# A decoder's last layer on flat tiles of 128 rows instead of 16 sequences of 112

## The reference

```
x = x + L1_attn(layernorm(x))
x = x + L1_xattn(layernorm(x), ctx)     # "wide attention"
x = x + L1_ffn(layernorm(x))            # "the MLP"

L1_xattn: q, k_new, v_new = x wq^T, x wk^T, x wv^T        (512 x 512 each)
          k = [ctx ; k_new], v = [ctx ; v_new]            (375 + 112 rows)
          softmax(q k^T / sqrt(512)) v wo^T               # one head, no mask
L1_ffn:   quant(W) = clip(round(W / s), -1, 1) * s,  s = mean|W| + 1e-8
          (silu(x Wup^T) * (x Wgate^T)) Wdown^T           # hidden width 2048
```

## Time and profile before

| | us |
|---|---|
| median of 3 runs | 3541.77 (3539.74 to 3544.45) |
| profiled execution, span from first to last instruction | 3554.0 |
| wide attention, one step | 19.1 |
| last DVE and POOL work of wide attention | ends 3192.99 |
| first DVE work of the MLP | 3193.34 |
| first block load of the MLP issued | 3199.74 |
| first up matmul of group 0, 1, 2, 3 | 3201.99, 3297.56, 3381.18, 3464.80 |
| last down begins | 3545.33 |

### The profile page before, as it was taken

One profiled execution on the slowest core, in us unless ns is written; L12 is line 12 of the kernel. 1 busy time (PEld: TensorE's weight loads), 2 busy tenths in 40 slices (PEclk: granted clock), 3 DMA queues, 4 the chain that ended last, 5 costly groups with the idle time before them and its releaser, 6 DMA issues. The chain is left out here.

```text
span 3554.0 us, 51327 instructions
## 1 busy us (share of the span) xinstructions
PE 3272.3 (92%) x17848; PEld 2662.8 (75%) x17848; DVE 2392.2 (67%) x6178; ACT 1727.0 (49%) x4171; POOL 794.8 (22%) x941
## 2 busy tenths in 40 slices
PE   5858999997999999999999988999889889988999
PEld 4647877885877877778788767888778667767887
DVE  5997878776666666766676665999655555558332
ACT  5975454444343344534433432888447655541222
POOL 0004444542222222422222213000413400000000
PEclk9879999999999999999999999999989989999999
DMA  6131010001000001100000026999700133423000
GB/s 232 30 67 25 1 48 24 1 36 66 23 26 23 23 23 50 68 21 21 30 21 23 18 92 213 390 400 400 272 22 2 48 125 121 123 88 107 11 10 21
DMA packets 117131, 297.27 MB, mean 84 GB/s; under 512 B 41888, under 2 KB 45472, under 8 KB 111120
## 3 DMA queue, kind: packets, MB, share of 16 engines
q1 hardware_dynamic: 110720, 276.39, 22.1%
q0 software_dynamic: 6160, 17.67, 1.6%
HBM read 251.65 MB, written 41.68 MB: 83 GB/s over the span
## 5 line engine op out<-in xcount | busy, mean ns | idle before, releaser
L42 PE MATMUL bank<-w,cross_ctx_part 128*125 128x512 f32 x1536 | 519.5, 419 | 2.8 <-DVE cross_kn L1176 2.8
L42 PEld LDWEIGHTS bank<-w,cross_ctx_part 128*125 128x125 f32 x1536 | 283.1, 187 | 84.4 <-DVE cross_kn L1176 8.7
L1084 ACT ACTIVATE cross_prob<-bank,cross_neg_max 112x375 f32<-112x375 f32 x256 | 147.3, 575 | 347.6 <-DVE cross_neg_max L1182 347.6
L42 PE MATMUL bank<-w_low,cross_ctx_part 128*125 128x512 f32 x768 | 303.0, 395 | 0.0
L1182 DVE TENSOR_REDUCE cross_neg_max<-bank 112x1 f32<-112x375 f32 x256 | 134.3, 526 | 208.8 <-PE bank L944 205.7
L42 PE MATMUL bank<-moe_wt,moe_zT 128*128 128x448 f32 x1176 | 263.7, 373 | 0.6 <-DVE moe_wt L1869 0.6
L1869 DVE TENSOR_TENSOR moe_wt<-moe_raw,moe_wt 128x1792 fp32r<-128x1792 f32 (+1 forms) x111 | 231.7, 2108 | 15.4 <-ACT moe_wt L1764 14.2
L42 PEld LDWEIGHTS bank<-moe_wt,moe_zT 128*128 128x128 f32 x1176 | 214.8, 189 | 15.9 <-DVE moe_wt L1869 0.8
L42 PE MATMUL bank<-mlp_zT,mlp_signs 128*128 128x448 f32 x1024 | 220.6, 368 | 5.6 <-DVE mlp_zT L2568 5.6
L42 PE MATMUL bank<-w,self_xq 128*128 128x512 f32 (+1 forms) x464 | 195.9, 422 | 23.0 <-DVE w_low L598 21.7
L42 PEld LDWEIGHTS bank<-mlp_zT,mlp_signs 128*128 128x128 f32 x1024 | 193.4, 189 | 27.3 <-issue 5.9
(11 more groups left out here) (433 smaller groups left out, 8171.8 us busy)
## 6 DMA issues: line engine op xcount, KB each, us to landing
moe_raw<-in_moe_w SPq DMA_DIRECT2D x74, 896.0 KB, 7.3
moe_raw<-in_moe_w SPq DMA_DIRECT2D x37, 1024.0 KB, 8.5
stream<-in_L1f SPq DMA_DIRECT2D x32, 768.0 KB, 4.2
cross_ctx_raw<-in_ctxT SPq DMA_DIRECT2D x32, 750.0 KB, 4.2
wide_ctxT<-in_ctxT SPq DMA_DIRECT2D x16, 750.0 KB, 4.2
wide_ctx_rows<-in_ctx SPq DMA_DIRECT2D x16, 750.0 KB
expert_rows<-a_zeros SPq DMA_DIRECT2D x1, 8960.0 KB, 25.7
moe_zrow<-expert_rows SPq DMA_DIRECT2D x35, 256.0 KB, 8.0
```

What stands on the lines that cost most here:

```text
L42: mm = pe.matmul(out, a, b, start=first and n == 0, stop=last and n == len(pairs) - 1)
L1084: op = act.activation(prob[:, t % SLOTS, i, :], score_bank(t)[0:S, i * NK:(i + 1) * NK], ACT.Exp, bias=neg_max[:, h:h + 1], accum_out=tota ...
```

## The change

1. Wide attention no longer measures sequences. SP stores each finished sequence to a tensor in device memory, `x5` of 1792 x 512 (`store_sequence`), and loads it back as tiles of 128 flat rows into slot t of `rows` (`load_tile`), as soon as the last sequence that a tile needs has landed. Tile t overwrites slot t, whose sequence is stored by then.
2. DVE measures tiles 0 to 9 in its steps 5 to 15 (`measure_tile`, three instructions on 128 partitions), four steps after the sequence that completes them. Tiles 10 to 13 (`LATE_TILES`) are measured in the MLP, group 1, step 2 (`measure_late`); POOL roots them there.
3. The MLP has groups of 4, 4, 4 and 2 tiles, that is 512, 512, 512 and 256 columns. Down has 2 matmuls per tile with weights of 128x128. The last store of a sequence and the loads of tiles 11 to 13 stand ahead of the block loads on SP's queue.
4. The loop over groups is written out on all engines, and x is stored as 14 tiles.

```diff
@@ new, beside the layers
+def last_sequence(t):
+    return (SLOT * t + SLOT - 1) // S
+def store_sequence(k, sp, x, b):
+    sp.dma_start(k.x5[S * b:S * (b + 1), :], x[0:S, b, :]).then_inc(k.rows_moved, 16)
+def load_tile(k, sp, x, t):
+    wait(sp, k.tile_landed[t % 2], 16 * (t // 2))
+    sp.dma_start(x[:, t, :], k.x5[SLOT * t:SLOT * (t + 1), :]).then_inc(k.tile_landed[t % 2], 16)
+def wait_tile(k, eng, t):
+    eng.wait_ge(k.tile_landed[t % 2], 16 * (t // 2 + 1))
+LATE_TILES = [t for t in range(NT) if last_sequence(t) + 4 >= B]
@@ wide_attention_layer, SP
                 load_mlp(b)
+                wait(sp, k.rows_moved, 16 * (b - 2))
+                for t in range(NT):
+                    if last_sequence(t) == b - 3:
+                        load_tile(k, sp, rows, t)
+                if b >= 2:
+                    sp.wait_ge(s["x_done"], b - 1)
+                    store_sequence(k, sp, rows, b - 2)
+            sp.wait_ge(s["x_done"], B - 1)
+            store_sequence(k, sp, rows, B - 2)
@@ POOL
-                pool.wait_ge(s["next_vareps"], b + 1)
-                pool.tensor_tensor(k.rstd[0:S, bass.ts(b, 1)], ve[:, bass.ts(b, 1)], k.half[0:S, 0:1], ALU.pow)\
-                    .then_inc(s["next_rooted"], 1)
+                for t in range(NT):
+                    if last_sequence(t) == b - 4:
+                        pool.wait_ge(s["next_vareps"], t + 1)
+                        pool.tensor_tensor(k.rstd[:, t:t + 1], ve[:, t:t + 1], k.half[:, 0:1], ALU.pow)\
+                            .then_inc(k.tile_rooted, 1)
@@ DVE
-            def measure_next(b):
-                dve.wait_ge(s["x_done"], b + 1)
-                dve.bn_stats(stats[:], x[:, b, :]).then_inc(s["next_stat"], 1)
...
+            def measure_tile(t):
+                wait_tile(k, dve, t)
+                dve.bn_stats(stats[:], rows[:, t, :]).then_inc(s["next_stat"], 1)
+                dve.wait_ge(s["next_stat"], t + 1)
+                dve.bn_aggr(k.mean_var[:, t, :], stats[:]).then_inc(s["next_centre"], 1)
+                dve.wait_ge(s["next_centre"], t + 1)
+                dve.tensor_scalar(ve[:, t:t + 1], k.mean_var[:, t, 1:2], EPS, None, ALU.add).then_inc(s["next_vareps"], 1)
...
-                if not first:
-                    measure_next(b - 1)
+                for t in range(NT):
+                    if last_sequence(t) == b - 4:
+                        measure_tile(t)
...
             add_out(B - 1)
-            measure_next(B - 1)
@@ ternary_mlp_layer
-    G = B // GB
+    G = (NT + GB - 1) // GB
+    def tiles_of(g):
+        return range(GB * g, min(GB * (g + 1), NT))
+    def width(g):
+        return P * len(tiles_of(g))
@@ PE: down, up and gate
-                for j in range(GB):
+                for j in range(len(tiles_of(g))):
                     if m == 0:
                         wait(pe, s["x_done"], GB * (g - 1) + j + 1)
-                    mm = product(pe, ps[4 + j][0:S, :], [t[:, m % 2, j * S:(j + 1) * S] for t in hT],
+                    mm = product(pe, ps[4 + j], [t[:, m % 2, j * P:(j + 1) * P] for t in hT],
                                  [signs[:, m, 2 * D:3 * D]], m == 0, m == MC - 1)
...
-                            mm = product(pe, ps[bank + m % 2][:, 0:N], [signs[:, m, at + c * P:at + (c + 1) * P]],
-                                         [t[:, c].rearrange("p b t -> p (b t)") for t in zT], c == 0, c == DC - 1)
+                            mm = product(pe, ps[bank + m % 2][:, 0:width(g)], [signs[:, m, at + c * P:at + (c + 1) * P]],
+                                         [t[:, c, 0:width(g)] for t in zT], c == 0, c == DC - 1)
@@ DVE
+            def measure_late():
+                for n, t in enumerate(LATE_TILES):
+                    wait_tile(k, dve, t)
+                    dve.bn_stats(stats[:, n, :], x[:, t, :]).then_inc(s["stat"], 1)
+                for n, t in enumerate(LATE_TILES):
+                    dve.wait_ge(s["stat"], n + 1)
+                    dve.bn_aggr(k.mean_var[:, t, :], stats[:, n, :]).then_inc(s["centre"], 1)
+                dve.wait_ge(s["centre"], len(LATE_TILES))
+                dve.tensor_scalar(ve[:], k.mean_var[:, LATE_TILES[0]:NT, 1], EPS, None, ALU.add).then_inc(s["vareps"], 1)
...
+                    if g == 1 and m == 2:
+                        measure_late()
@@ POOL, SP
+            pool.wait_ge(s["vareps"], 1)
+            pool.tensor_tensor(k.rstd[:, LATE_TILES[0]:NT], ve[:], k.half[:, 0:len(LATE_TILES)], ALU.pow)\
+                .then_inc(k.tile_rooted, len(LATE_TILES))
...
+            store_sequence(k, sp, x, B - 1)
+            sp.wait_ge(k.rows_moved, 16 * B)
+            for t in LATE_TILES:
+                if last_sequence(t) > B - 4:
+                    load_tile(k, sp, x, t)
             for m in range(MLP_SLOTS, MC):
                 sp.wait_ge(s["sign"], 3 * (m - MLP_SLOTS) + 3)
...
-            with sp.Fori(0, B) as b:
-                sp.wait_ge(s["x_done"], b + 1)
-                sp.dma_start(io["out"][b], x[:, b, :]).then_inc(s["x_stored"], 16)
+            for t in range(NT):
+                sp.wait_ge(s["x_done"], t + 1)
+                sp.dma_start(out[SLOT * t:SLOT * (t + 1), :], x[:, t, :]).then_inc(s["x_stored"], 16)
@@ decoder
-        wide_attention_layer(k, x, io, stream, magnitudes)
-        ternary_mlp_layer(k, x, io, stream, magnitudes)
+        wide_attention_layer(k, x, rows, io, stream, magnitudes)
+        ternary_mlp_layer(k, rows, io, stream, magnitudes)
```

More of the change, by code:

```diff
@@ L61, in __init__ @@
         self.ctx_landed = ctx.enter_context(nc.semaphore("ctx_landed"))
+        self.rows_moved = ctx.enter_context(nc.semaphore("rows_moved"))
+        self.tile_landed = [ctx.enter_context(nc.semaphore(f"tile_landed{i}")) for i in range(2)]
+        self.tile_rooted = ctx.enter_context(nc.semaphore("tile_rooted"))
         self.all_sems = ctx.enter_context(ExitStack())
@@ L2059, in second_attention_layer, with wide_attention_layer @@
         k.next_stage()
-def wide_attention_layer(k, x, io, stream, magnitudes):
+def last_sequence(t):
[8 more added lines that the diff above has]
+LATE_TILES = [t for t in range(NT) if last_sequence(t) + 4 >= B]
+def wide_attention_layer(k, x, rows, io, stream, magnitudes):
     nc, ps = k.nc, k.ps
@@ L2465, in ternary_mlp_layer, with over_loop @@
         half = k.sb(ctx, "mlp_half_scale", [P, 2, 3], F32)
-        z = k.sb(ctx, "mlp_z", [S, GB, D], F32)
-        zT = [k.sb(ctx, f"mlp_zT{i}", [P, DC, GB, S], F32R) for i in range(2)]
-        silu = k.sb(ctx, "mlp_silu", [P, 2, GB * S], F32)
-        h = k.sb(ctx, "mlp_h", [P, 2, GB * S], F32)
-        hT = [k.sb(ctx, f"mlp_hT{i}", [P, 2, GB * S], F32R) for i in range(2)]
-        block = ctx.enter_context(nc.Block())
-        N = GB * S
-        def over_loop(eng, step):
-            step(0, True)
-            with eng.Fori(1, G - 1) as g:
-                step(g, True)
-            step(G - 1, False)
+        z = k.sb(ctx, "mlp_z", [P, GB, D], F32)
+        zT = [k.sb(ctx, f"mlp_zT{i}", [P, DC, GB * P], F32R) for i in range(2)]
+        silu = k.sb(ctx, "mlp_silu", [P, 2, GB * P], F32)
+        h = k.sb(ctx, "mlp_h", [P, 2, GB * P], F32)
+        hT = [k.sb(ctx, f"mlp_hT{i}", [P, 2, GB * P], F32R) for i in range(2)]
+        stats = k.sb(ctx, "mlp_stats", [P, len(LATE_TILES), 6], F32)
+        ve = k.sb(ctx, "mlp_ve", [P, len(LATE_TILES)], F32)
+        block = ctx.enter_context(nc.Block())
+        def over_loop(step):
+            for g in range(G):
+                step(g, g + 1 < G)
         def raw(m, n):
@@ L2527, in _ @@
             pe.wait_ge(s["mean_ready"], 1)
-            over_loop(pe, step)
+            over_loop(step)
         @block.scalar
@@ L2542, in high @@
                         act.wait_ge(s["y_in_psum"], MC * g + m - 1)
-                    act.activation(hT[0][:, m % 2, :], h[:, m % 2, :], ACT.Copy).then_inc(s["h_high"], 1)
+                    act.activation(hT[0][:, m % 2, 0:width(g)], h[:, m % 2, 0:width(g)], ACT.Copy).then_inc(s["h_high"], 1)
                 for m in range(MC):
@@ L2547, in step @@
                     act.wait_ge(s["up_in_psum"], MC * g + m + 1)
-                    act.activation(silu[:, m % 2, :], ps[m % 2][:, 0:N], ACT.Silu, scale=neg_scale[:, 0:1])\
+                    act.activation(silu[:, m % 2, 0:width(g)], ps[m % 2][:, 0:width(g)], ACT.Silu, scale=neg_scale[:, 0:1])\
                         .then_inc(s["silu_ready"], 1)
@@ L2554, in _ @@
             z_high(0)
-            over_loop(act, step)
+            over_loop(step)
         @block.vector
@@ L2584, in low @@
                     dve.wait_ge(s["h_high"], MC * g + m + 1)
-                    dve.tensor_tensor(hT[1][:, m % 2, :], h[:, m % 2, :], hT[0][:, m % 2, :].bitcast(F32),
-                                      ALU.subtract).then_inc(s["h_low"], 1)
-                first = isinstance(g, int) and g == 0
+                    dve.tensor_tensor(hT[1][:, m % 2, 0:width(g)], h[:, m % 2, 0:width(g)],
```

(2 more changed lines are left out.)

56 lines of the change are left out of this document (27 added, 29 removed).

## The result

The changed kernel takes 3519.89 us (median of 4 runs, 3518.53 to 3524.73), the kernel before 3541.13 (3539.74 to 3544.45): ratio 0.9939, 95% interval 0.9928 to 0.9951. That is 21.2 us less; the forecast was 20.9 less, 3520.9.

The account below looks back on a forecast made before the run. PE was taken to bound wide attention and MLP groups 1 to 3, DVE's loop group 0. Terms -1.8, +0.2, +2.4, +1.0, +7.3, +6.2, -34.2, -2.0 sum to -20.9 us: 3541.8 becomes 3520.9, range 3513 to 3530.

Parts of the forecast that it names:

- Step 1: Between the layers: the last sequence's statistics and POOL's root leave the path, -1.8 us.
- Step 2: Wide attention: fewer DVE measurements give no gain, added stores and loads are covered by a step of slack; 0 us.
- rival B: Wide attention: transfers on SP's queue hold up steps 3 to 15, 5.2 us each, +68 us, 3589; 4%.
- Step 3: Start of the MLP: z_low on four tiles is longer, tile loads end in time or nearly so; +0.2 us.
- Step 4: MLP group 0: DVE's loop goes from 5.68 to 5.85 us, +2.4; the last two steps are PE's, +1.0.
- Steps 5 and 6: MLP groups 1 and 2, PE-bound: 512-column matmuls cost 0.0268 us more each; +7.3 and +6.2 us.
- Step 7: MLP group 3: 256-column up and gate -20.0, half the down matmuls -14.8, one PE wait of 0.6; -34.2 us.
- Step 8: The end: two last adds instead of four, -1.5, and one chain at 256 columns, -0.5; -2.0 us.
- The offset of 12.2 us: Profiled span 3554.0 us above the runs' median; taken as the profiled execution's own and carried over.
- Rival A: Group 3: weight loads set the pace, +16.6 us, 3537.5, 4%; load and stream one after the other, 3565, 1%.
- C: Opening of the MLP costs more through PE's slower clock, a late block and PE binding group 0; +6, 3527; 12%.
- D: More is won: wide attention -5, 128-column weights load no slower, boundary shorter by 1 to 2; 3514; 8%.

Follow-up runs that it names:

- measured_at_end: Changed kernel with the statistics of tile 9 taken after the last add_out instead of in step 15; ratio 0.9951 to the kernel before.
- no_moves: Changed kernel without its stores to and loads from device memory and without their waits; ratio 0.9945 to the kernel before.
- moves_twice: Changed kernel with its moves through device memory doubled, all waited for; ratio 0.9943 to the kernel before.
- late_in_group_0: Changed kernel with the statistics of the four late tiles in group 0, step 2, instead of group 1, step 2; ratio 0.9942 to the kernel before.
- small_group_first: Changed kernel with MLP groups in the order 2, 4, 4, 4 tiles; ratio 1.0026 to the kernel before.
- before_written_out: Kernel before with only the loop over the MLP's groups and the loop of stores written out; ratio 1.0006 to the kernel before.
- stores_of_112_rows: Changed kernel with final stores of 112 rows of each tile instead of 128; one run, 3519.34 us.
- one_tile_last: Changed kernel without tile 13 in the last layer, so its last group has one tile and 128-column up and gate matmuls; one run, 3509.93 us.

## Why the prediction was right

The forecast of 3520.9 us was met by 3519.89, and by its own steps. It counts a group from its first up matmul, the table above from its first h. In the changed kernel the first up matmuls stand at 3185.05, 3284.07, 3375.57 and 3466.01; cut there, group 0 is 3.45 us longer than before, group 1 7.9, group 2 6.8, and group 3 up to the last adds 35.75 shorter. The steps are held against these.

- Step 1, the statistics between the layers: -1.8 forecast, -1.85 read. Shown by measured_at_end (+1.66 when put back).
- Step 2, wide attention unchanged: right, shown by no_moves and moves_twice. The landing time in it was mis-sized, 2.6 instead of 11.8 us, and with it rival B's price; its cover held.
- Step 3, start of the MLP: +0.2, read +0.3. SP issued the last tile load at 3182.97 and the first block load at 3183.34, 0.8 us after the signs of block 0; no step of group 0 was longer for it.
- Step 4, group 0: +3.4 forecast, +3.45 read. DVE's loop is 5.86 us for 5.67; the four steps with a normalisation, which the forecast didn't tell apart, are 6.31 for 6.12, the same +0.19. That DVE sets this stage is shown by late_in_group_0 and small_group_first.
- Steps 5 and 6, groups 1 and 2: +13.5 forecast, +14.7 read. Each 512-column matmul was 0.0013 us dearer than forecast and a down matmul with 128 weight columns 0.0026, in all about 1.3 us over the two groups. (The table has +13.5 only because its cut puts the first sixteen matmuls of group 3, which got cheaper, into group 2.) The statistics of the late tiles, 2.9 us of DVE, hid in group 1.
- Step 7, group 3 with step 8's chain: -34.7 forecast, -35.75 read. A matmul of 256 columns at 0.119 instead of 0.1263 and a stall of 0.33 instead of 0.6 us gave 2.2 us more than reckoned. Some 1 us of it was given back at the last step: the down of four matmuls ahead of the last one no longer covers the chain to the last low part, and PE waits 0.56 us before the last down (at 3511.70 above) where it waited 0.19. From the last but one down to the last it is 1.65 us after 2.21, -0.56, where the forecast had counted the shorter down and the shorter chain both, -1.4.
- Both sizes could have been had beforehand. The 0.1263 came by taking 12 x 0.2312 off the whole series of the earlier trace rows, but there the twelve matmuls of 512 columns take from 63.62 to 66.47, 0.2375 each, as the first alone takes 0.34; the twelve of 256 columns, read by themselves, take 1.44 us, 0.120 each. And the chain's terms for the stall, 2.98 + 0.50 + 0.42 + 0.44, come to 4.34 us and not to 4.6, which makes the stall 0.3. PE in order of time, from the first 256-column matmul of that series on, in the kernel before:

```profile
66.47 1.59 PE L42 MATMUL bank<-a_qkv,a_zT 128*128 128x256 f32 x12
67.91 0.39 PE L42 MATMUL bank<-a_o,a_oT 128*128 128x512 f32 x1
```

- Step 8, the end: -1.5 for the adds against -2.7 (-2.6 with the ends of the spans read to 0.01 us). The traces close this sum: the adds give 1.32 us (2.73 to 1.41), the time from the last add to the last store's issue 0.75 (0.78 to 0.03; before_written_out has 0.03 too), and that store's landing 0.54 (2.59 to 2.04; stores_of_112_rows has 2.54). The last two the forecast had left out.
- The offset of 12.2 us between span and median, which I called the profiled execution's own, has nothing to do with profiling: the profiled execution of the changed kernel was a run of 3518.53 us with a span of 3516.8. So the profiled execution of the kernel before was itself longer than the median. Its trace alone can't say where, but the code ahead of wide attention ends up to 21 us apart between profiles.

That the total came within 1 us is in part luck. By stages the misses were +1.2 in groups 1 and 2, -1.0 in group 3, -1.1 at the end and, in the profiled execution, +1.6 from the clock at the last projection, and they cancel. The mechanism was right at each step, and the term that carried the forecast was right to 3%.

Rival A (weight loads set the pace in group 3) was refuted by 0.119 us a matmul; one_tile_last, with loads at 0.112, shows how near it was. The Trainium skill's rule that a load overlaps matmuls in flight only at other row groups ("TensorE: Matmul & The Clock Gate", "Packing small matmuls — row/col tiling") doesn't hold for these loads: load and stream of the same row group overlap at 512 and 256 columns, where 0.2325 and 0.119 us a matmul leave 0.019 and 0.012 beside the columns at 2.4 GHz, and a load shows 0.19. The Trainium skill's price of 1/1.2 ns a column on the same page (section "LDWEIGHTS (loading the stationary operand)"), 107 ns for 128 columns, is near the pace of 112 ns that these loads have in one_tile_last. Rival B was refuted by no_moves and moves_twice, C and D by the stages.

## What to carry to other kernels

When rows are grouped anew, count matmuls and not only columns: the columns of up and gate stayed the same, and the gain was in the down matmuls whose number follows the number of row blocks, not in their size. Then ask of each stage which engine sets it, since the same edit cost 2.8 us in one group and nothing in the next, and the same groups in another order lost 30 us. A detour through device memory was free here because a whole step, 19 us, lies between its issue and its use and it lands in 11.8; read its landing time behind the transfers that stand ahead of it in the queue, not from an idle one. And read the price of a matmul shape from the starts of that shape alone, not as the rest of a mixed series.

## What the runs showed of the hardware that was not expected

- The time of a matmul in a series is 0.2325 us at 512 columns, 0.2044 at 448, 0.174 at 384 and 0.119 at 256, that is 19, 18, 14 and 12 ns above the columns at 2.4 GHz, so the forecast's constant of 18 ns is too much for narrow ones. A line of 5.5 ns plus 0.443 ns a column, fitted to these four, meets each to 1.5 ns. At 128 columns it would give 62 ns; the 112 measured are the pace of the weight loads.
- The same code ahead of wide attention ends between 2851.7 and 2872.8 us in fourteen profiles. Up to ACT's copy of the expert layer's gate weights, at 2101.0 to 2103.7, they agree to 3 us; by the first softmax of the second attention, behind the expert layer, they are at 2620.0 to 2637.9. From 2000 to 2400 us DMA is busy 0.65 of the time in the kernel before and 0.67 after, and most of the 21 us arises between these two points. What makes an execution longer or shorter in it was not looked for.
- POOL's comparison over 128x512, 1.78 us, makes a DVE instruction beside it 1.06 instead of 0.75 us long.
- A store of 128 partitions landed in 2.1 us and one of 112 in 2.6 (medians). Of four stores of 112 in a row the first takes 2.25 us and the fourth up to 2.94, those of 128 all take 2.0 to 2.1.
